# Mamba-2 scan with gated experts on one core: scans issued two at a time in odd steps

## The reference

```
proj = xn @ in_proj_w.T                       # gate 8192, x 8192, B and C 1024 each, dt 128
xBC  = silu(conv1d(xBC, 4 taps) + conv_b)
dt   = clip(softplus(dt + dt_bias)); dA = dt * A; cs = cumsum(dA) per chunk of 128 tokens
scores = (C @ B^T) * exp(cs_l - cs_s) where l >= s            # per head
y    = scores @ (x * dt) + state carried between chunks + x * D
yg   = y * silu(gate);  rstd = rsqrt(mean(yg^2 over a group of 1024) + eps)
s    = (yg * rstd * norm_w) @ out_proj_w.T
out  = x + s * silu(experts(xn))              # 16 experts, the best two of each token
```

## Time and profile before

| | us |
|---|---|
| median of 3 runs | 1605.9 |
| lowest and highest | 1604.34 and 1606.1 |
| the profiled execution, its own time | 1605.15 |
| its span in the trace | 1603.2 |
| PE busy | 1588.8 (99%) |
| DVE busy | 1409.1 (88%) |
| ACT busy | 1196.3 (75%) |
| POOL busy | 961.7 (60%) |

### The profile page before, as it was taken

One profiled execution on the slowest core, in us unless ns is written; L12 is line 12 of the kernel. 1 busy time (PEld: TensorE's weight loads), 2 busy tenths in 40 slices (PEclk: granted clock), 3 DMA queues, 4 the chain that ended last, 5 costly groups with the idle time before them and its releaser, 6 DMA issues.

```text
span 1603.2 us, 28456 instructions
## 1 busy us (share of the span) xinstructions
PE 1588.8 (99%) x8478; PEld 1267.1 (79%) x8478; DVE 1409.1 (88%) x1654; ACT 1196.3 (75%) x2305; POOL 961.7 (60%) x596
## 2 busy tenths in 40 slices
PE   9999999999999999999999999999999999999998
PEld 6888777887778777887778777887778777877776
DVE  7727899889999899889998899889998899889987
ACT  4525878777787878777787878777787878778772
POOL 6523456655666556655666556655666666656563
PEclk9999999999999999999999999999999999999999
DMA  5234344334443344344443334334443334334442
GB/s 187 75 136 148 126 137 169 118 131 143 146 140 118 127 129 169 121 129 143 148 140 118 127 129 170 121 127 144 145 139 122 127 128 163 129 122 149 151 133 85
DMA packets 83831, 216.88 MB, mean 135 GB/s; under 512 B 10576, under 2 KB 12880, under 8 KB 83536
## 3 DMA queue, kind: packets, MB, share of 16 engines
q1 hardware_dynamic: 83376, 214.55, 39.7%
q10 hardware_dynamic: 288, 0.30, 0.1%
HBM read 209.83 MB, written 4.98 MB: 134 GB/s over the span
## 4 chain that ended last, share of the span: by engine, by line
PE 84%; DVE 8%; ACT 3%; issue 3%; POOL 1%; DMA 0%; SPq 0%; ACTq 0%; DVEq 0%; POOLq 0%
PE pj L454 15%; PE pj L456 14%; PE pj L455 14%; PE pr L454 9%; PE pr L455 7%; PE pr L456 7%; PE sc L699 7%; PE sc L703 3%; PE tb L688 3%; DVE conv L1375 3%; ACT decay L967 1%; DVE wo_lo L1439 1%; DVE xc L1389 1%; PE tb L712 1%; DVE decay L1403 1%
## 5 line engine op out<-in xcount | busy, mean ns | idle before, releaser
L1079 POOL TENSOR_TENSOR w_lo<-stg,w_hi 128x512 fp32r<-128x512 f32 x316 | 496.6, 1572 | 314.5 <-ACT w_hi L941 253.0
L454 PE MATMUL pj<-xT_hi,w_hi 128*128 128x512 f32 x1208 | 476.3, 394 | 4.4 <-DVE conv L1375 1.5
L456 PE MATMUL pj<-xT_hi,w_lo 128*128 128x512 f32 x1208 | 470.8, 390 | 0.0
L455 PE MATMUL pj<-xT_lo,w_hi 128*128 128x512 f32 x1208 | 470.4, 389 | 0.0
L1375 DVE SCALAR_TENSOR_TENSOR conv<-pj,par,conv 128x510 f32<-128x510 f32 (+2 forms) x480 | 357.8, 745 | 76.2 <-ACT conv L949 63.0
L967 ACT ACTIVATE decay<-decay,dtg 128x256 f32<-128x256 f32 (+1 forms) x1024 | 378.9, 442 | 0.0
L1116 POOL TENSOR_TENSOR xc<-xc,thg 128x512 f32<-128x512 f32 x128 | 203.2, 1587 | 188.2 <-DVE xc L1426 187.6
L1122 POOL TENSOR_TENSOR sqsum<-sqsum,sq 128x512 f32<-128x512 f32 x112 | 216.8, 1936 | 115.4 <-ACT sq L995 112.2
L454 PEld LDWEIGHTS pj<-xT_hi,w_hi 128*128 128x128 f32 x1208 | 226.8, 188 | 59.7 <-issue 9.4
L456 PEld LDWEIGHTS pj<-xT_hi,w_lo 128*128 128x128 f32 x1208 | 226.8, 188 | 48.0
L455 PEld LDWEIGHTS pj<-xT_lo,w_hi 128*128 128x128 f32 x1208 | 226.9, 188 | 45.3
(11 more groups left out here) (182 smaller groups left out, 1976.5 us busy)
## 6 DMA issues: line engine op xcount, KB each, us to landing
stg<-wstream SPq DMA_DIRECT2D x387, 256.0 KB, 2.7
decay<-cs_scr SPq DMA_DIRECT2D x128, 768.0 KB, 4.3
acc<-hid SPq DMA_DIRECT2D x8, 256.0 KB, 5.2
out<-acc SPq DMA_DIRECT2D x8, 256.0 KB, 2.0
dt_scr<-decay SPq DMA_DIRECT2D x1, 1024.0 KB, 6.4
gate_scr<-part SPq DMA_DIRECT2D x4, 256.0 KB, 2.0
dtg<-dt_scr SPq DMA_DIRECT2D x16, 64.0 KB, 4.0
stg<-hid SPq DMA_DIRECT2D x4, 256.0 KB, 4.7
```

The source lines that it names most:

```text
L454: nc.tensor.matmul(dst, hi_w, hi_x, start=first, stop=False)
L455: nc.tensor.matmul(dst, hi_w, lo_x, start=False, stop=False)
L456: return nc.tensor.matmul(dst, lo_w, hi_x, start=False, stop=last)
L1079: nc.gpsimd.tensor_tensor(w_dest(n, 1), stg[:, s % RING, :], f32(w_dest(n, 0)), ALU.subtract).then_inc(S["wl"], 1)
```

## The change

The scans of an even step s-1 and of the odd step s are now both done in step s, one right after the other. To let the second begin before the first one's result is fetched, scan results go to the banks `yb`: even ones to `sc`, odd ones to `tb`, `pr[0]` or `pr[3]`, and a scan waits for `add_scan` of two before. This brings waits for those banks: `scan(1)` for the mean square, `scan(3)` for `add_output` 0, `scan(5)` and `scan(7)` for all four. `x_turn(2)` goes to the end of step 1, since `tb` is the bank of `scan(1)`.

The other engines follow. SP loads exponents for two pairs in even steps. ACT raises the decays of pair s+1 in step s (before: of s+2), has `tap` ahead of the late clearings and the exp, and does `y_hi` and `square` of two pairs in even steps, the second square last. DVE makes both `block_weights` of a pair of scans in the even step, one behind `x_times_dt`, one near the end, and both `add_scan` in the odd step; `add_output` 3 goes from the end to the start of step 5. POOL does two `gated` in odd steps and two `add_square` in even ones.

The core of the diff follows. Of ACT's `step` only the lines that stand there now are shown.

```
@@ -214,6 +214,9 @@
         sc = psum("sc", [P, H])
         tb = psum("tb", [P, H])
         ob = pr[3]
+        yb = [sc, tb, sc, pr[0], sc, pr[3], sc, pr[3]]
...
@@ -388,8 +391,10 @@
             def step(g, half, s):
                 for i in range(len(pieces(g, half, s))):
                     load_piece(g, half, s, i)
-                if has_pair(g, half, s + 3):
-                    load_exponents(*pair(g, half, s + 3))
+                for n in (s + 2, s + 3):
+                    if s % 2 == 0 and has_pair(g, half, n):
+                        load_exponents(*pair(g, half, n))
...
@@ -684,6 +689,9 @@
                 pe.wait_ge(S["silu"], at(g, half, NX, j + 3))
                 pe.wait_ge(S["ms"], at(g, half, 1, 0 if j >= 2 else -1))
                 pe.wait_ge(S["xdt"], at(g, half, NJ, j))
+                if j == 2:
+                    pe.wait_ge(S["u"], at(g, half, NJ, 2))
                 for t in range(4):
                     mm = nc.tensor.transpose(tb[:, t * P:(t + 1) * P], xc[:, j, t * P:(t + 1) * P], ident)
                 mm.then_inc(S["xt"], 1)
@@ -691,16 +699,22 @@
             def scan(g, half, j):
                 pe.wait_ge(S["w"], at(g, half, NJ, j + 1))
                 pe.wait_ge(S["xdt"], at(g, half, NJ, j + 1))
-                pe.wait_ge(S["u"], at(g, half, NJ, j))
+                pe.wait_ge(S["u"], at(g, half, NJ, j - 1))
+                if j == 1:
+                    pe.wait_ge(S["ms"], at(g, half, 1, 0))
+                elif j % 2 == 1:
+                    pe.wait_ge(S["acc"], at(g, half, 4, 1 if j == 3 else 4))
+                if j == 5:
+                    pe.wait_ge(S["fg"], NTT)
                 for b in range(2):
                     c0 = 2 * b * P
                     for h in range(2):
                         hd = slice(h * HD, (h + 1) * HD)
-                        nc.tensor.matmul(sc[hd, c0:c0 + 2 * P], xdt[:, j % 2, 2 * b, hd],
+                        nc.tensor.matmul(yb[j][hd, c0:c0 + 2 * P], xdt[:, j % 2, 2 * b, hd],
                                          decay[:, j % NDEC, 2 * h + b, 0:2 * P], start=True, stop=False)
                     for h in range(2):
                         hd = slice(h * HD, (h + 1) * HD)
-                        mm = nc.tensor.matmul(sc[hd, c0 + P:c0 + 2 * P], xdt[:, j % 2, 2 * b + 1, hd],
+                        mm = nc.tensor.matmul(yb[j][hd, c0 + P:c0 + 2 * P], xdt[:, j % 2, 2 * b + 1, hd],
                                               decay[:, j % NDEC, 2 * h + b, 2 * P:3 * P], start=False, stop=True)
                 mm.then_inc(S["y"], 1)
...
@@ -725,6 +739,9 @@
                     if half == 0:
                         pe.wait_ge(S["ol"], oindex(g, 4))
                 pe.wait_ge(S["acc"], at(g, half, 4, t + 1))
+                if t in (0, 3):
+                    pe.wait_ge(S["u"], at(g, half, NJ, 4 if t == 0 else NJ))
...
@@ -756,14 +773,17 @@
                     channel_block(g, half, mine[0])
                 if s == 5 and not is_last(g, half):
                     bc_products(*following(g, half))
-                if has_pair(g, half, s + 1):
+                if s != 1 and has_pair(g, half, s + 1):
                     x_turn(*pair(g, half, s + 1))
-                if has_pair(g, half, s):
+                if s % 2 == 1 and has_pair(g, half, s):
+                    scan(g, half, s - 1)
                     scan(g, half, s)
                 if len(mine) > 1:
                     channel_block(g, half, mine[1])
                 if with_out:
                     out_of_step(g, half, s)
+                if s == 1:
+                    x_turn(*pair(g, half, s + 1))
...
@@ -995,50 +1015,55 @@
...
                 nc.scalar.activation(sqsum[:, :] if j == 0 else sq[:, :], xc[:, j, :], ACT.Square).then_inc(S["sq"], 1)
             def step(g, half, s, with_out=True):
+                before = (g, 0) if half == 1 else (g - 1, 1)
                 fill = isinstance(g, int) and g < 0
+                gated = ("g", s) in blocks(g, half, s)
+                mine = [b[1] for b in blocks(g, half, s) if b[0] == "x"]
+                todo = list(range(len(pieces(g, half, s))))
+                raised = has_pair(g, half, s + 1)
+                done = []
+                if s == 0 and with_out:
+                    done = [(*before, NJ - 2), (*before, NJ - 1)]
+                elif s >= 2 and s % 2 == 0 and has_pair(g, half, s - 1):
+                    done = [(g, half, s - 2), (g, half, s - 1)]
+                if gated and todo:
+                    split(g, half, s, todo.pop(0))
+                if raised and not fill:
+                    drops(*pair(g, half, s + 1), 0)
+                if gated:
                     gate_tanh(g, half, s)
+                if done:
+                    y_hi(*done[0])
+                if mine:
+                    tap(g, half, mine[0])
+                if todo:
+                    split(g, half, s, todo.pop(0))
                 if fill and s == 4:
                     expert_hi(13)
+                if done:
+                    y_hi(*done[1])
+                    square(*done[0])
+                if raised and fill:
+                    drops(*pair(g, half, s + 1), 0)
+                if raised:
+                    drops(*pair(g, half, s + 1), 1)
+                if raised and s % 2 == 1:
+                    decays(*pair(g, half, s + 1))
                 if mine:
+                    x_tanh(*of_half(g, half, mine[0]), mine[0])
+                for m in mine[1:]:
+                    tap(g, half, m)
+                if todo:
+                    split(g, half, s, todo.pop(0))
+                if raised and s % 2 == 0:
+                    decays(*pair(g, half, s + 1))
+                for m in mine[1:]:
+                    x_tanh(*of_half(g, half, m), m)
+                if done:
+                    square(*done[1])
+                while todo:
+                    split(g, half, s, todo.pop(0))
             for s in range(4, NJ):
                 step(-1, 1, s, False)
...
@@ -1127,14 +1153,19 @@
                 if n:
                     split_low(g, half, s, 0)
                 if with_out and s == 0:
-                    add_square(*before, NJ - 1)
+                    add_square(*before, NJ - 2)
                 if with_out and s == 2:
                     inverse_rms(*before)
-                if s >= 2 and has_pair(g, half, s):
-                    add_square(g, half, s - 1)
+                if s >= 4 and s % 2 == 0 and has_pair(g, half, s):
+                    add_square(g, half, s - 2)
                 for i in range(1, n):
                     split_low(g, half, s, i)
-                if has_pair(g, half, s):
+                if with_out and s == 0:
+                    add_square(*before, NJ - 1)
+                if s >= 2 and s % 2 == 0 and has_pair(g, half, s):
+                    add_square(g, half, s - 1)
+                if s % 2 == 1 and has_pair(g, half, s):
+                    gated(g, half, s - 1)
                     gated(g, half, s)
             for s in range(4, NJ):
...
@@ -1455,49 +1487,61 @@
             def step(g, half, s, with_out=True):
                 before = (g, 0) if half == 1 else (g - 1, 1)
+                fill = isinstance(g, int) and g < 0
                 mine = [b[1] for b in blocks(g, half, s) if b[0] == "x"]
+                even = s % 2 == 0
+                done = []
+                if s == 0 and with_out:
+                    done = [(*before, NJ - 2), (*before, NJ - 1)]
+                elif s >= 2 and even and has_pair(g, half, s - 1):
+                    done = [(g, half, s - 2), (g, half, s - 1)]
                 if half == 0 and s == 0 and not (isinstance(g, int) and g == 0):
                     channel_parameters(g)
                 if half == 1 and s == 4 and not isinstance(g, int):
                     conv_parameters(g + 1)
                 if with_out and s == 1 and half == 0:
                     mean_square(*before)
+                if with_out and s == 5:
+                    add_output(*before, 3)
                 if has_pair(g, half, s):
                     gate_silu(g, half, s)
-                if has_pair(g, half, s + 1):
-                    block_weights(*pair(g, half, s + 1))
                 if mine:
                     taps(g, half, mine[0])
-                if isinstance(g, int) and g < 0 and s == 4:
+                if fill and s == 4:
                     expert_weighted(13)
                 if s == 5 and not is_last(g, half):
                     mask_products(*following(g, half))
-                if has_pair(g, half, s + 1):
+                if even and has_pair(g, half, s + 1):
                     x_times_dt(*pair(g, half, s + 1))
-                if has_pair(g, half, s):
+                if not even and has_pair(g, half, s):
+                    add_scan(g, half, s - 1)
                     add_scan(g, half, s)
+                if not even and s != 1 and has_pair(g, half, s + 1):
```

(29 more changed lines are left out.)

50 lines of the change are left out of this document (7 added, 43 removed).

## The result

The changed kernel took 1712.5 us (median of 4 runs, 1706.1 to 1717.6) against 1606.0 for the kernel before on the same chip. The ratio is 1.066, 95% interval 1.0643 to 1.0677. The forecast was 1653 with a range of 1612 to 1680: the sign was right, and the loss is more than twice what the sum gave. The profiled execution of the changed kernel took 1706.13 us, at a mean granted clock of 0.984; before it was 0.999. The runs of one kernel now lie 11 us apart, where those of before lie 1 to 5 apart.

A forecast was written before the change was run, and what follows sets the result against it. PE was taken as the bound, busy for all 90.3 us of a half. The terms -22 + 37 + 28 + 4 = +47 on the profiled 1605.15 us gave 1652, or 1653 against the median of 1605.9; range 1612 to 1680.

The forecast's parts named there:

- the tail: Behind the loop: y_lo(6) stands behind scan(7), but PE has two output parts (5.4 us) meanwhile; cost nothing.
- Part 4: The rest: scan(3) and scan(7) waiting for DVE's weights or add_output, mostly hidden; 4 us on both (0 to 9).
- Part 1: Scans in pairs on PE save turns between matmul forms, 0.35 us per pair, 64 pairs; -22 us.
- Part 2: PE's square_sums in step 1 waits for squares now behind decays on ACT; 2.5 us at 15 places, +37 us.
- Part 3: PE's bc_products in step 5 waits for add_output(2), now behind weights on DVE; mean 2.0 us, 14 places, +28 us.
- the bound that the forecast had set: Part 1 would be wrong if PE's passage between the two scans exceeded 0.1 us.
- the signs that the forecast named: PE idle some 70 us, at square sums and bc products; two-scan clusters about 3.4 us; two halves some 187 us.
- the upper end: Part 3's wait if POOL blocks DVE most: 2.5 us in half 1, 3.7 in half 0; +0.8 was taken instead.
- scan(7) is alike: In Part 4, scan(7) was taken to be like scan(3): hidden, up to 0.6 us late when POOL blocks twice.
- in twos: nothing: Exponent loads two at a time come a step and more ahead of ACT, so they cost nothing.
- Rival (a): Only the squares make PE wait, since DVE gets its weights ahead of time; 1621 us, chance 0.13.
- rival (b): Faster: the orders fit, both waits are hidden and only the turns are left; 1584 us, chance 0.09.

The follow-up runs named there:

- e11_scan_first: e9_order with DVE's two add_scan of step 1, half 1, ahead of the convolution block's taps; 1591.2 us.
- e3_loads: Changed kernel with SP loading the exponents of one pair in every step, not two pairs in even steps; 1724.2 us.
- e10_order_loads: e9_order with the changed kernel's exponent loads, two pairs at a time in even steps; 1614.5 us.
- e2_addout: Changed kernel with add_output(2) in DVE's step 4 ahead of wo_lo, the second silu and the odd pair's decay multiply; 1716.2 us.
- e8_b_square: Kernel before the change with only ACT's last square of step 0 moved to the end of its work; 1633.8 us.
- e4_three: Changed kernel with step 0's squares and their sums earlier, add_output(2) earlier in step 4, and exponent loads one pair per step; 1655.5 us.
- e5_weights_tail: e4_three with DVE's even-pair decay multiply at the head of even steps, and step 7 ahead of the first final sums behind the loop; 1630.1 us.
- e9_order: e5_weights_tail with ACT's last step-0 square behind the tap, add_output(3) ending step 4, odd-pair multiply ahead of wo_lo in even steps but 4; 1598.0 us.
- e6_weights: Changed kernel with only DVE's multiply of the even pair's decays moved to the head of the even step; 1700.6 us.

## Why the sum was too small, step by step

Two steps of the prediction failed. It priced each wait at its length and had no term for the clock, which cost 23.7 us; and it took the second scans and the tail as hidden (Part 4, 4 us for all), where 22.0 came. The other terms were off by 3 to 7 us each.

| term | forecast | measured |
|---|---|---|
| Part 1, turns | -22 | -19.0 |
| Part 2, square_sums | +37 | +40.4 |
| Part 3, bc_products (with the wait behind the jump) | +28 | +34.6 |
| Part 4, second scans, for weights or add_output | +4 | +16.0 |
| tail | 0 | +6.0 |
| other waits, beyond those of before | 0 | -0.7 |
| half clock | not in the sum | +23.7 |
| sum | +47 | +101.0 (spans: 100.8) |

**Part 1: sign right, size nearly so.** A cluster with two scans, in the changed kernel:

```profile
674.51 0.60 PE L696 MATMUL tb<-cst,xc 128*128 128x128 f32 x4
675.03 0.65 PE L713 MATMUL sc<-decay,xdt 128*64 128x256 f32 x4
...
676.17 0.39 PE L717 MATMUL sc<-decay,xdt 128*64 128x128 f32 x4
676.38 0.60 PE L713 MATMUL pr<-decay,xdt 128*64 128x256 f32 x4
...
677.78 0.50 PE L459 MATMUL pr<-wo_hi,yT_hi 128*128 128x512 f32 x1
678.12 0.39 PE L460 MATMUL pr<-wo_lo,yT_hi 128*128 128x512 f32 x1
```

674.51 to 678.12 less one product is 3.38, and 3.39 was forecast. Over the loop the medians from start to start are: transposes to scan 0.203 us, scan to product 0.203, the last matmul of one scan to the first of the next 0.103, and a lone cluster of transposes to products 0.028. Before, a pair of steps paid 2 x (0.203 + 0.203) = 0.812; now 0.028 + 0.203 + 0.103 + 0.203 = 0.537, so 0.275 is saved. Single rows give 4.18 - 0.44 - 3.38 = 0.36, since they also hold the first block of a scan behind transposes, which is slower (0.48 instead of 0.43) and which these medians leave out; so the sum below is rather low. The passage of 0.103 is at the bound that the forecast had set: it is not the full turn, and it is what neighbouring token blocks inside a scan pay as well (0.102). In step 1, where the transposes stand apart, the passage from a product into the first scan takes 0.318 where a product would follow after 0.227, and the pair pays 0.318 - 0.227 + 0.103 + 0.203 + 2 x 0.028 = 0.453 instead of 0.812: 0.36 is saved. 48 x 0.275 + 16 x 0.36 = 19.0, and 19.1 in e11_scan_first. By the rule of the Trainium skill's page "TensorEngine Tiling (Array Packing)", section "Key Properties", the second scan pays no drain; the trace agrees, since its passage costs the same 0.10 as one without a change of bank.

Of the signs that the forecast named, these came: the idle time of PE rose (by 96 us, not 70), the two kinds of wait have the releasers and lengths named, and the period of two halves grew (to 192.4, not 187).

**Part 2: right in place, mechanism and size.** ACT in step 0 of half 0, and POOL:

```profile
735.80 0.78 ACT L969 ACTIVATE conv<-pj,par 128x512 f32<-128x512 f32 x1 [1.69 <-PE pj L461]
...
739.74 1.48 ACT L995 ACTIVATE decay<-decay 128x1536 f32<-128x1536 f32 x1
741.12 0.61 ACT L1015 ACTIVATE sq<-xc 128x512 f32<-128x512 f32 x1
```

```profile
739.56 2.79 POOL L1105 TENSOR_TENSOR w_lo<-stg,w_hi 128x512 fp32r<-128x512 f32 x1
742.31 1.71 POOL L1148 TENSOR_TENSOR sqsum<-sqsum,sq 128x512 f32<-128x512 f32 x1
```

From the tap's start to the square's end are 5.93 us; the forecast's own items from there are 0.66 + 0.52 + 0.52 + 0.52 + 1.17 + 0.53 + 1.39 + 0.62 = 5.93. POOL came to it 0.6 us late, from its own split, and the sum took 1.7. The wait was 2.7 a place in both halves, against 2.5 taken (the sum gave 1.6 to 2.6 in half 0 and 2.2 to 3.3 in half 1).

**Part 3: right, once the jump is counted with it.** Alone, bc_products gave 20.2, under the forecast. Since e3_loads moves 14.4 us from the jump to this place without changing the sum, the delay is 34.6 us against 28, at 14 places 2.5 us instead of 2.0. In half 0 some 2.5 came where 2.6 was taken, in half 1 2.1 where 1.4 was. The forecast had taken +0.8 for POOL's blocking; the row of half 1 that made the difference:

```profile
696.02 2.84 DVE L1435 TENSOR_TENSOR decay<-decay,gm 128x1536 f32<-128x1536 f32 x1
698.79 0.74 DVE L1484 SCALAR_TENSOR_TENSOR acc<-pr,rstd,acc 128x512 f32<-128x512 f32 x1
```

The multiply took 2.84 where the sum had 1.65, so in half 1 the upper end was nearer. Over the whole program the 128 multiplies took 266.2 us, 2080 ns in the mean; 241.2 and 1885 before (other instructions of DVE gained, x_silu most: its mean fell from 1552 ns to 943). In both kernels those that no POOL instruction overlaps take 1.74 to 1.75 us, and all longer ones have POOL at work beside them. The new order puts 88 of the 128 beside more than 1.2 us of POOL's work, the old one 66.

**Part 4: the step that failed among the waits.** "Hidden, up to 0.6 late when POOL blocks twice" gave 4 us, and 16.0 came. scan(3) waits some 0.5 us in half 0, as said; scan(7) waits some 1.3, eight times. "scan(7) is alike" skipped the count: by the view of waits these 8 places are the decay multiply itself (8.6 us). DVE ahead of it, step 6 of half 0:

```profile
625.80 1.35 DVE L1471 SCALAR_TENSOR_TENSOR wo_lo<-stg,par,wo_hi 128x512 fp32r<-128x512 f32 x1 [0.50 <-ACT wo_hi L957]
627.07 1.77 DVE L1421 SCALAR_TENSOR_TENSOR xc<-thx,conv 128x512 f32<-128x512 f32 x1
628.76 1.75 DVE L1435 TENSOR_TENSOR decay<-decay,gm 128x1536 f32<-128x1536 f32 x1
```

From start to start wo_lo took 1.27 and the silu 1.69 where the sum has 0.60 for each, and wo_lo had waited 0.50 for ACT's wo_hi: 2.3 us in one row of work, where "up to 0.6 late" had allowed two blockings against slack. In the tail the two output parts of PE did not cover y_lo: PE waited 6.0 us, since the gate's product and add_scan of step 7 stood behind four instructions of the final sums, and y_lo behind four more. And the loads "in twos: nothing" was argued from ACT's side only, whether data would be there in time. It never asked what else is carried by the DMA engines at that moment. In the changed kernel that costs nothing net, in e10_order_loads it costs 16.5 us.

**What was missing altogether: the clock.** Of the 54 us by which the spans differ more than forecast, 23.7 are half-clock stretches, the largest single part. The profile before shows PE busy for all of 90.3 us at clock 1.00 and can't show what idle time does to the clock; but every wait in the sum was a wait of an engine that had not waited before, and I priced it at its length. The Trainium skill's page "TensorE: Matmul & The Clock Gate", section "What's actually happening", says that TensorE's clock is halved when the engine has been idle. The rows above agree as to the two levels, and in the loop stretches at half clock come only at waits. The forecast had 29 waits of 2 to 2.5 us. At the 1.5 us that a stretch costs, one behind each is up to 43 us, a rival of its own at some 1695; in the share that came, 14 of 32, it is 19 us. No such rival was among them.

**And what a sum of waits can't do.** The experiments show the terms of such a sum to be coupled in both directions. Taken away one at a time, waits of 20.2 us were worth nothing that the scatter lets one see and waits of 40.4 were worth 30, since DVE was late for the next place as well. Taken away together they gave more than the sum of each alone, in part since the clock came back with them. Rival (a), squares only, was wrong about DVE; rival (b) has the right sum for a different order: 1584 forecast, 1591 reached by e11_scan_first, in which the scans are paired and the waits in the loop are hidden.

The scatter goes with the clock too. The median of the changed kernel lies 6.4 us above its profiled execution, and its runs lie 11 us apart: 1706.1 us at a mean granted clock of 0.984, 1712.1 at 0.981, 1712.9 at 0.979, 1717.6 at 0.975. In e2_addout 1704.7 us had 0.983 and 1727.7 had 0.969. One stretch of 3.41 us at half clock lowers the mean of such a run by 0.001, so 0.009 less is an estimated 9 stretches more, 1.3 us each. Why their number changes from run to run stays open, since the stretches themselves are seen in the profiled execution only.

## What to carry to other kernels

When an engine that never waits is made to wait, price the wait at more than its length: 2 us at the square sums of e8_b_square cost about 3.5, because the granted clock fell behind them, and in the changed kernel 14 of 32 waits of this kind had such a stretch behind them. When work is reordered on helper engines, look for their idle stretches and put first what is already ready, and don't judge an edit by undoing it alone: the waits before the second scans, of 0.5 to 1.8 us, stood behind those of 2 to 3 us, and showed only when these were gone. A transfer that is "early enough" for its reader can still hurt whoever shares the DMA engines with it, the loop's own jump included (16.5 us in e10_order_loads).

## What the runs showed of the hardware

- Waits of TensorE of 1.7 to 2.7 us inside dense work are often followed, mostly within 2 us, by a stretch of 3.41 us at a granted clock of 0.50 that costs about 1.5 us. At the square sums: 7 of 7 in e8_b_square, 10 of 15 in the changed kernel. Elsewhere less often: 2 of 8 at bc_products and 1 of 6 behind the jump in the changed kernel, 1 of 6 behind the jump in e10_order_loads, none of the seven of 1.7 us before scan(5) in e4_three. Waits of 1.35 us at the square sums of e5_weights_tail had one 4 times in 8, those of 0.8 us before x_turn(2) in e9_order none in 8.
- A loop's compare-and-branch on TensorE's sequencer that jumps back takes 3.3 to 5.0 us with single loads of 768 KB, mostly covered by queued matmuls, and 5.7 to 6.8 with two of them issued just ahead of it (3.7 to 5.9 in e6_weights, also with two); the last one, which falls through, takes 0.1. A 16 KB packet of an instruction queue lies in each of the long ones, and they end 1.3 to 1.5 us behind its end (e3_loads, e6_weights, e9_order, e10_order_loads and the changed kernel).
- A DVE multiply of 128x1536 with two inputs takes 1.75 us alone and up to 2.87 beside POOL's 128x512 instructions; POOL's own 1.27 us instructions take up to 2.8 in the same stretches.
- From the last 128*64 matmul of a scan to the first of the next, in another bank, 0.103 us pass; from 128*128 to 128*64 and back 0.203 each way, and 0.318 from 128x512 products into a scan. Transposes to products, both 128*128, take 0.028.
